# Opening of a fused ViT tower kernel: what is loaded first, where the second image row stands in the load queue, and who scales it

## What is computed

```python
h = tok(x)        # 5 channel pairs: the image and its 4 shifts by (+-4, +-4); one mean and variance per
                  # image over all 5 pairs; normed * gamma + beta; then an 8x8 patch convolution, + b
h = concat([cls_tok, h])                       # 169 patches + 1 class token, width 128, 64 images
q, k, v = Wq @ LN(h), Wk @ LN(h), Wv @ LN(h)   # x (64, 2, 104, 104)
S_t = S_{t-1} + 0.01 * v_t k_t^T               # summed over the batch; starts at memory0
h = h + S_t q_t                                # scan over tokens
h = h + LN(h)                                  # the last stage, where its mask leaves the input as it is
```

## Time and profile before

| | |
|---|---|
| median of three executions | 230.68 us |
| profiled execution, device time | 230.59 us |
| its span, first to last instruction | 228.8 us |
| mean granted TensorE clock | 0.975 |
| busy: TensorE / VectorE / ScalarE / GpSimd | 201.1 / 156.4 / 111.9 / 158.0 us |
| time moved by DMA | 26.00 MB in the whole, 15.73 MB of it in the first 62 us |

### The profile page before, as it was taken

How to read it: one execution, slowest core, us unless ns; L and a number is a source line. 1 busy time by engine, 2 the same in 40 slices (tenths; PEclk the granted TensorE clock), 3 DMA queues, 4 the chain that set the end, 5 groups by cost and what they waited for, 6 DMA issues and landing times.

```text
span 228.8 us, 4922 instructions
## 1 busy us (share of the span) xinstructions
PE 201.1 (88%) x1558; PEld 170.5 (75%) x1558; DVE 156.4 (68%) x765; ACT 111.9 (49%) x243; POOL 158.0 (69%) x124
## 2 busy tenths in 40 slices
PE   0299999899899999999999999999999999967720
PEld 0289898778688899888888888898888888856510
DVE  2558992351576796597778769577748967878882
ACT  6002211345334564665556576467467556665460
POOL 1039789899982999959999489489998225333340
PEclk9999999999999999999999999999999999999955
DMA  6999957913112005061062512201201220121235
GB/s 169 371 428 422 422 224 115 382 59 112 46 37 122 3 0 194 18 202 46 3 199 48 180 24 46 49 9 41 46 3 46 47 50 1 44 50 46 46 71 122
DMA packets 16543, 26.00 MB, mean 114 GB/s; under 512 B 1319, under 2 KB 13277, under 8 KB 16262
## 3 DMA queue, kind: packets, MB, share of 16 engines
q1 hardware_dynamic: 16108, 25.31, 34.5%
q10 hardware_dynamic: 410, 0.38, 0.5%
HBM read 19.77 MB, written 5.92 MB: 112 GB/s over the span
## 4 chain that ended last, share of the span: by engine, by line
PE 74%; POOL 9%; DMA 5%; DVE 4%; ACT 3%; issue 2%; SPq 1%; DVEq 0%; ACTq 0%; POOLq 0%
PE conv L473 36%; PE vr_ps L513 13%; PE first_ps L526 9%; PE outs L546 9%; POOL scaled L397 7%; DMA wt<-weight 3%; PE turn L505 3%; PE conv L479 2%; ACT values L649 2%; DMA out<-images 1%; POOL g_low L966 1%; PE second_ps L585 1%; PE turn L585 1%; DVE state L755 1%; DVE state L747 1%
## 5 line engine op out<-in xcount | busy, mean ns | idle before, releaser
L473 PE MATMUL conv<-scaled,wt 128*128 128x256 f32 (+3 forms) x460 | 116.8, 375 | 10.1 <-DMA wt<-weight 10.1
L397 POOL TENSOR_TENSOR scaled<-rows,gam 128x832 f32<-128x832 f32 x60 | 93.8, 1586 | 6.0 <-PE conv L473 6.0
L473 PEld LDWEIGHTS conv<-scaled,wt 128*128 128x128 f32 x460 | 77.7, 194 | 18.4 <-DMA wt<-weight 10.1
L649 ACT ACTIVATE values<-vr_ps,rstd 128x256 f32<-128x256 f32 x85 | 40.3, 475 | 70.5 <-PE vr_ps L513 59.6
L976 POOL TENSOR_TENSOR rstd<-var,powers 128x8 f32<-128x8 f32 (+2 forms) x22 | 33.7, 1530 | 31.4 <-DVE var L767 31.4
L747 DVE TENSOR_TENSOR state<-first_ps,state 128x128 f32<-128x128 f32 x83 | 24.2, 291 | 31.1 <-PE first_ps L526 25.5
L657 ACT ACTIVATE images<-images,ln_shift,ln_gain 128x128 f32<-128x128 f32 x81 | 38.3, 484 | 5.3 <-DVE ln_shift L811 3.1
L513 PE MATMUL vr_ps<-w_high,g_low 128*128 128x256 f32 x85 | 34.1, 401 | 3.8 <-ACT values L649 3.8
L966 POOL TENSOR_TENSOR g_low<-g_t,g_high 128x512 fp32r<-128x512 f32 (+1 forms) x22 | 27.2, 1236 | 6.4 <-ACT g_high L636 6.4
L736 DVE BATCH_NORM_STATS2 ln_stats<-images 128x6 f32<-128x128 f32 x85 | 23.7, 284 | 6.7 <-ACT images L643 6.5
L755 DVE TENSOR_TENSOR state<-second_ps,state 128x128 f32<-128x128 f32 x82 | 23.2, 283 | 2.5
(11 more groups left out here) (116 smaller groups left out, 219.4 us busy)
## 6 DMA issues: line engine op xcount, KB each, us to landing
rows<-x_windows SPq DMA_DIRECT2D x13, 864.0 KB, 5.7
out<-images SPq DMA_DIRECT2D x42, 128.0 KB, 2.4
images<-x_rows SPq DMA_DIRECT2D x3, 624.0 KB, 20.7
images<-x_rows SPq DMA_DIRECT2D x1, 1456.0 KB, 13.2
images<-x_rows SPq DMA_DIRECT2D x1, 1248.0 KB, 15.6
images<-x_rows SPq DMA_DIRECT2D x1, 832.0 KB, 19.7
small<-smalls SPq DMA_DIRECT2D x1, 512.0 KB, 8.7
terms<-parked SPq DMA_DIRECT2D x3, 168.0 KB
```

The lines of the kernel that those rows point to most:

```text
L397: return eng.tensor_tensor(scaled[:, s, at:at + N], window, gains, ALU.mult)
L473: last = pe.matmul(conv_ps[g % 2][:, at:at + n * B], wt[:, s], scaled[:, s, a % RING:a % RING + n], start=first, stop=(g < EARLY and s == ...
L649: act.activation(values[:, t % VALUE_SLOTS].rearrange("p a e -> p (a e)"), vr_ps[:, 0:2 * E], ACT.Identity, scale=rho_of(t)).then_inc(vr_r ...
```

## The change

- SyncE: the gammas of patch row 0 come as an array of their own (`first_gamma`, 5 x 13 per partition, 32.5 KB), then the aligned windows of row 0, the weights, the other windows of row 0 with a semaphore of their own, the first offset windows, gamma, beta, `small`, row 1, image parts 0 to 2, row 2, parts 3 and 4. After row 0 is scaled: row 3, then parts 5 and 6. There are seven image parts instead of six.
- TensorE: 14 products of zeros (`WARM`) in front of the wait for the weights. The tables stand in front of the three small products; group 1 in front of the class token's product; shifts 0 to 3 of group 3 in front of `image_sums`; shifts 0 and 1 of group 4 in front of the product that waits for `scale_cols`.
- ScalarE: takes over the subtraction of means in the three small matrices and a copy of the class token from VectorE; copies the high halves of the tables first; and scales shift 4 of rows 2 and 3 (`scale_here`), with 13 instructions of 64 columns each.
- GpSimd: the class token's power stands behind row 1; shift 4 of rows 2 and 3 is left out.
- VectorE: loses those small operations; `w_low` is made after part 1 instead of part 0, straight from PSUM.

```diff
-STAT_CHUNKS = [(0, 28), (28, 24), (52, 12), (64, 16), (80, 12), (92, 12)]
+WARM = 14
+STAT_CHUNKS = [(0, 16), (16, 16), (32, 20), (52, 16), (68, 16), (84, 8), (92, 12)]
+BY_SCALAR = ((2, 4), (3, 4))
...
+            sp.dma_start(gam_first[:], first_gamma).then_inc(first_gamma_in, 16)
+            sp.dma_start(rows[:, 0, 0:N], x_windows[:, 0, 0:N]).then_inc(row_in[0], 16)
+            sp.dma_start(wt[:], weight).then_inc(weight_in, 16)
+            sp.dma_start(rows[:, 0, N:2 * N + 1], x_windows[:, 0, N:2 * N + 1]).then_inc(first_right_in, 16)
+            sp.dma_start(rows[:, ROW_SLOTS - 1, N:2 * N + 1], first_offsets).then_inc(first_offsets_in, 16)
             sp.dma_start(gam[:], gamma).then_inc(gamma_in, 16)
-            load_row(0)
-            sp.dma_start(rows[:, ROW_SLOTS - 1, N:2 * N + 1], first_offsets).then_inc(first_offsets_in, 16)
-            sp.dma_start(wt[:], weight).then_inc(weight_in, 16)
+            sp.dma_start(bet[:], beta).then_inc(beta_in, 16)
             sp.dma_start(small[:], smalls).then_inc(small_in, 16)
             load_row(1)
-            sp.dma_start(bet[:], beta).then_inc(beta_in, 16)
             load_images(0)
             load_images(1)
+            load_images(2)
             load_row(2)
-            for i in range(2, len(STAT_CHUNKS)):
-                load_images(i)
+            load_images(3)
+            load_images(4)
 
             sp.wait_ge(scaled_first, SHIFTS)
             load_row(3)
+            load_images(5)
+            load_images(6)
...
+            pe.wait_ge(zeros_ready, 1)
+            for _ in range(WARM):
+                pe.matmul(out_ps[:, 0:E], zeros[:], zeros[:], start=True, stop=True, skip_group_check=True)
             pe.wait_ge(weight_in, 16)
             conv_shifts(0, 0, SHIFTS)
...
+            conv_shifts(1, 0, SHIFTS)
             pe.wait_ge(cls_t_ready, 1)
             pe.wait_ge(w_vr_ready, 2)
             pe.matmul(vr_ps[:, 0:2 * E], cls_t[:], w_vr[:], start=True, stop=True).then_inc(vr_done, 1)
-            conv_shifts(1, 0, SHIFTS)
+            conv_shifts(2, 0, SHIFTS)
             pe.wait_ge(vr_ready, 1)
...
-            conv_shifts(2, 0, SHIFTS)
-            conv_shifts(3, 0, 3)
+            conv_shifts(3, 0, 4)
             pe.wait_ge(sums_ready, 2)
+            pe.wait_ge(w_low_ready, 1)
             pe.matmul(out_ps[:, 2 * E:2 * E + 2], small[:, SAME], sums[:], start=True,
                       stop=True).then_inc(image_sums_done, 1)
-            conv_shifts(3, 3, SHIFTS)
+            conv_shifts(3, 4, SHIFTS)
+            conv_shifts(EARLY - 1, 0, EARLY_SHIFTS)
             pe.wait_ge(scale_cols_ready, 1)
...
+            def scale_here(r, s):
+                act.wait_ge(row_in[r % ROW_SLOTS], 16)
+                act.wait_ge(gamma_in, 16)
+                act.wait_ge(conv_step, SHIFTS * last_group_of_row(r - 2) + s + 1)
+                offsets = (r if s < 3 else r - 1) % ROW_SLOTS
+                right = N + (s - 1) % 2
+                for j in range(N):
+                    last = act.activation(scaled[:, s, r % 2 * N + j], rows[:, offsets, right + j], ACT.Identity,
+                                          scale=gam[:, s, r * N + j:r * N + j + 1])
+                last.then_inc(scaled_by_scalar, 1)
```

More of the change, by code:

```diff
@@ L169, with pool_scales @@
 EARLY_ROWS = 4
+BY_SCALAR = ((2, 4), (3, 4))
+def pool_scales(r, s):
+    return SHIFTS * (r - 1) + s + 1 - len([at for at in BY_SCALAR if at <= (r, s)])
 FIRST_SCALES = (-7, -5, -4, -3, -2)
@@ L183, with tower @@
 LATE_SCALES = [(r, s, scale_step(r, s)) for r in range(EARLY_ROWS, N) for s in range(SHIFTS)]
-def tower(nc, x_rows, x_windows, first_offsets, gamma, beta, weight, smalls, cls_tok, out, parked):
+def tower(nc, x_rows, x_windows, first_offsets, first_gamma, gamma, beta, weight, smalls, cls_tok, out, parked):
     with ExitStack() as ctx:
@@ L377, in wait_scaled @@
                 eng.wait_ge(scaled_first, s + 1)
-            if last > 0:
-                eng.wait_ge(scaled_rows, SHIFTS * (last - 1) + s + 1)
+            if (last, s) in BY_SCALAR:
+                eng.wait_ge(scaled_by_scalar, BY_SCALAR.index((last, s)) + 1)
+            elif last > 0:
+                eng.wait_ge(scaled_rows, pool_scales(last, s))
         def wait_group(eng, g):
@@ L572, in _ @@
             pe.wait_ge(small_in, 16)
[L573 to L577, removed]
             pe.wait_ge(gamma_in, 16)
@@ L591, in _ @@
                 last.then_inc(tables_done, 1)
+            pe.wait_ge(centered, 3)
+            pe.matmul(out_ps[:, 0:E], wk_c[:], wq_c[:], start=True, stop=True, skip_group_check=True)
+            pe.matmul(out_ps[:, E:2 * E], center[:], small[:, WV], start=True, stop=True,
+                      skip_group_check=True).then_inc(products_done, 1)
+            pe.matmul(first_ps[:, 0:E], wq_c[:], small[:, MEM], start=True, stop=False, skip_group_check=True)
+            conv_shifts(1, 0, SHIFTS)
             pe.wait_ge(cls_t_ready, 1)
@@ L689, in _ @@
             act.copy(terms[:], zeros[:].unsqueeze(1).to_broadcast([P, GROUPS, E])).then_inc(terms_zero, 1)
+            act.wait_ge(cls_in, 32)
+            act.wait_ge(cls_padded, 1)
+            act.copy(cls_t[:, B:P], cls_col[:].to_broadcast([P, B])).then_inc(cls_t_ready, 1)
+            act.wait_ge(small_in, 16)
+            act.wait_ge(ones_ready, 1)
+            act.activation(center[:], small[:, IDENT], ACT.Identity, bias=powers[:, 11:12]).then_inc(centered, 1)
+            act.wait_ge(weight_means_ready, 3)
+            for i, (w, dst) in enumerate(((WQ, wq_c), (WK, wk_c))):
+                act.activation(dst[:], small[:, w], ACT.Identity, bias=w_minus[:, i:i + 1]).then_inc(centered, 1)
             act.wait_ge(scale_cols_zero, 1)
             group_out(0)
+            for blk, ps in enumerate((turn_ps, second_ps)):
+                count = P if blk == 0 else PATCHES - P
+                act.wait_ge(tables_done, blk + 1)
+                act.copy(term_parts[0:count, blk, :, 0],
+                         ps[0:count, 0:2 * E].rearrange("p (k e) -> p k e", e=E)).then_inc(table_high_ready, 1)
             act.wait_ge(products_done, 1)
@@ L872, in _ @@
                 dve.bn_stats(w_stats[:, i], small[:, w]).then_inc(weight_stats_done, 1)
-            dve.tensor_scalar(center[:], small[:, IDENT], -1.0 / E, None, ALU.add).then_inc(centered, 1)
             dve.wait_ge(weight_stats_done, 2)
@@ L877, in _ @@
             dve.wait_ge(weight_means_ready, 2)
[L878 to L879 removed]
+            dve.tensor_scalar(w_minus[:], w_mv[:, :, 0], -1.0, None, ALU.mult).then_inc(weight_means_ready, 1)
             dve.wait_ge(cls_in, 32)
[L881 to L882 removed]
             dve.bn_stats(ln1_stats[:, 0], cls_h[:]).then_inc(ln1_stats_ready, 1)
@@ L1009, in _ @@
                 for s in range(SHIFTS):
+                    if r == 2 and s == 0:
+                        pool.wait_ge(consts_ready, 2)
+                        pool.wait_ge(ln1_var_ready, 1)
+                        pool.tensor_tensor(cls_rho[:], cls_var[:], powers[:, 0:1], ALU.pow).then_inc(rho_ready, 1)
                     if r == EARLY_ROWS - 1 and s == 2:
@@ L1013, in _ @@
                                            ALU.pow).then_inc(image_power_ready, 1)
-                    scale(r, s)
+                    if (r, s) not in BY_SCALAR:
+                        scale(r, s)
             for t in range(START, affine_step(GROUPS - 1)):
@@ L1049 @@
         "first_offsets": offsets[:, 0],
+        "first_gamma": windows(gamma.reshape(SHIFTS, 2, S, S))[:, :, 0],
         "gamma": windows(gamma.reshape(SHIFTS, 2, S, S)).reshape(P, SHIFTS, PATCHES),
```

55 lines of the change are left out of this document (27 added, 28 removed).

## The result

The changed kernel takes 235.36 us (median of four executions, 234.49 to 235.74) against 230.80 us for the kernel before on the same chip; the ratio is 1.0192, with a 95% interval of 1.0165 to 1.0220. It is 1.9% slower. The forecast was 233.8 us within 230.2 to 235.8. The profiled execution, the slowest of the four, took 235.74 us with a span of 233.5 us, where the one before had 230.59 and 228.8.

A forecast was written before the change was run, and what follows sets the result against it. TensorE bounds the dense middle, so the forecast is the shift of `early(0)` added to 230.6: late statistics 0.6, half-rate clock 2.8 + 0.4, together 3.8, taken as +3.2 for a rise on the way: 233.8 us, range 230.2 to 235.8.

The forecast's parts named there:

- (d): Rival: clock stays at half rate beyond `early(0)`, where TensorE is nearly full; 2 us more, 235.8; chance 0.08.
- The loads: Opening's load queue at 413 KB per us: last image part lands at 33.5, where it was 30.8.
- The floor by `terms`: `early(0)` not before about 41: one engine carries the 41-partition store, so `terms` lands at 41.0 +-0.3 again.
- The gap and the clock: TensorE idle 32.1 to 36.8 before `image_sums`, clock falls to half rate: 2.8 + 0.4 us, up to 1 saved.
- Late statistics and order: From last image part to `early(0)`: 41.7, 0.6 us later than before, if TensorE runs at full rate.
- The hidden parts: Opening work beside other work: ScalarE's scaling, 3.2 us, costs nothing and GpSimd's saving is worth nothing; first zeros 5.9 us.
- (a): Rival: late statistics with the clock held through the gap before `image_sums`; +0.6, 231.2 us; chance 0.20.
- (c): Rival: last image part lands at 31.8, `terms` decides; 230.6, no change; chance 0.10 with (e), both without loss.
- (e): Rival: products of zeros don't lift the clock; group 0 up to 2.9 us later, nothing at the end; 0.10 with (c).
- (b): Rival: whole load queue starts sooner, from 3 to 4 us of start; 229.9 if 1.3 us sooner; chance 0.14.

The follow-up runs named there:

- c2_row3_last_fill: Changed kernel with row 3 loaded after image parts 5 and 6, and 14 products of zeros before the wait for the sums: 232.52 us, ratio 1.0058.
- c4_first_zeros: Kernel before with only the 14 products of zeros at its start: 230.70 us, ratio 1.0001.
- a2_fill_gap: Changed kernel with 22 more products of zeros in front of the wait for the sums: 231.79 us, ratio 1.0011.
- a5_fill_split: Changed kernel with row 3 loaded last, the 41-partition store cut into 32 and 9, and 14 products of zeros before the sums wait: 234.47 us, ratio 1.0136.
- b1_row3_before_last: Kernel before with row 3 issued in front of the last image part: 232.30 us, ratio 1.0029.
- c3_split_store_again: Kernel before with its 41-partition store cut into 32 and 9, same kernel as `b2_split_store`, more rounds: 230.52 us, ratio 0.9971.
- b2_split_store: Kernel before with its 41-partition store cut into 32 and 9: 229.83, 229.93, 233.51 and 233.66 us, ratio 0.9965 from the lower two.

## Why the prediction was right

The mechanism up to `early(0)` is the one that was forecast, and the time lies in the range. But the range reached 235.8 for the sake of (d), a clock that stays low beyond `early(0)`, and that did not happen: it was 0.95 from 42 to 45. The 1.6 us above the forecast lie in two places at which the sum had nothing: the end of the kernel, and the time outside the span, which is 2.1 to 2.2 us in the four executions of the changed kernel against the 1.8 that the forecast carried over. That the measured time still fell inside the range is luck.

**The loads.** The last image part at 33.5: measured 33.64. `small` at 12.4 (VectorE used it at 12.64) and row 1 at 14.5 (GpSimd at 14.87) were close. Row 2 at 23.1 was 1.4 us off: GpSimd began it at 24.49, behind a wait for the load. So loads in the middle of the queue can lag behind the mean rate too, not only the last. The weights, forecast at 6.2, were used at 6.98, and group 0 ended at 13.1 instead of 12.3. None of this cost anything, since TensorE reached the sums at 31.9 (forecast 32.1) all the same.

**The floor by `terms`.** Right, and shown twice: the wait for the stores ended at 35.06 (35.13 before), and where the rest was early (`c2_row3_last_fill`, `c4_first_zeros`) `early(0)` waited for `terms`. The split store moved it.

**The gap and the clock.** Gap 4.7 us forecast, 5.12 measured. Fall of the clock: right. Its price was 2.8 + 0.4 in the sum and up to 1 less for a rise on the way, 2.6 as taken; measured 2.4.

**Late statistics and order.** Forecast 0.6, measured 0.88 (41.99 in `a2_fill_gap`), of which the order is 0.6.

**The hidden parts.** ScalarE's 13 scalings took 3.21 us, forecast 3.2, and are worth nothing, as said. The first zeros took 5.14 us instead of 5.9: TensorE got through 7 records of them in the microsecond from 4 to 5 and 11 in the next, so the full rate came before they ended. In `c4_first_zeros` they took 6.32.

**The rivals.** None came true. The clock did not hold, against (a); the last image part landed at 33.6 and not at 31.8, against (c); the clock rose again before `early(0)`, against (d); and the products of zeros did reach the full rate, against (e). For (b) the queue as a whole would have had to start sooner, but `small` was used at 12.64, no sooner than the rate from the rows gives. The 3 to 4 us of start that (b) names should read 4.4: 8.2 less 3.1 less the issue at 0.74.

**What the sum lacked** is the end. +3.2 was forecast for `early(0)` and +3.29 measured, but the span grew by 4.7, and 0.4 us more lie outside it. I had written that nothing later could add time. The clock can: in the traced execution of the changed kernel it also fell between 209 and 220, and 1.4 us were lost where TensorE is thinly used in both kernels. I had also misread: TensorE's busy tenths in the last five slices are 6, 7, 7, 2 and 0, so the thin part begins at 200 us, two slices sooner than I wrote. The mechanism was in the rows that I used for the opening, and I did not apply it to the place where I had read it. The other three executions of the changed kernel have spans of 232.4 to 233.4 us, so if the opening took its 3.3 us from each, they lost 0.3 to 1.3 us there. Why the clock falls there in some executions and not in others stays open; no run here varied the end alone, and none shows that the change has to do with it.

## What to carry over

When work is moved ahead of a wait for data, ask what TensorE will do during the wait: here a lead of 4.6 us became a gap of 5.1 us, and the gap cost 2.4 us by the clock, while the lead by itself could give nothing as long as `terms` landed at 41. Reorder a load queue by the slack of each consumer, the last place above all, and find the transfer that holds the rest back before speeding up the engines in front of it. Two faster pieces are not additive when they share a queue: the store that gained 0.9 us in one kernel cost about 2 us in the other (`early(0)` at 43.84 against 41.71, medians 234.47 against 232.52).

## What the runs showed of the hardware

- TensorE's granted clock fell within or just behind a gap of 5.1, 4.3, 3.5 and even 2.8 us, and products of zeros in place of the gap kept it at 1.00 in the three traces that have 22 of them. The length of one gap does not settle it: it fell between 40 and 41 in `a5_fill_split` behind gaps of 1.69 and 0.41 us, and it stayed at 1.00 in `c2_row3_last_fill`, where TensorE was busy for 1.2 of the 4 us from 38 to 42 with no gap over 1.5 us.
- It also falls near the end, in stretches where TensorE is busy 4.1 of 6 us, in some traces and not in others: 0.88 and 0.78 in the changed kernel, 1.00 in `a2_fill_gap` (231.35 us in that execution) and in the kernel before. From a state of the opening that is the same to 0.1 us, the span was 228.8 us in the trace of the kernel before and 232.6 in that of `c4_first_zeros`, with the clock at 0.51 from 205 to 217 in the latter.
- The granted clock in the profile does not show the half rate at the start: it reads 1.00 from 11 to 13 us in the kernel before, where 6 records of group 0 fill the 2 us, as many as in `c4_first_zeros` at a clock of 0.50. The same group, begun within 0.3 us of the same time, took 6.23, 6.79, 7.37 and 7.54 us in four traces without products of zeros in front of it (`b1_row3_before_last`, `c3_split_store_again`, the kernel before, `b2_split_store`).
- Loads of `terms` that run beside row loads bring the rate down to 126 GB/s at a share of 1.30, and the load of row 3, issued 17 us earlier on the same queue, was used 3.6 us later than where they came behind it (37.30 against 33.72).
